# Attention in a four-layer decoder stack: value products of eight heads as one step, a 96-wide turned shift, and a mask taken by VectorE's minimum

## What is computed

```python
# layer 0: causal self-attention, cross-attention, feed-forward (1024)
# layer 1: causal self-attention, cross-attention, mixture of 8 experts, top 2
# layer 2: self-attention with a mask given as input, cross-attention, feed-forward
# layer 3: cross-attention
def _mha(x, ctx, wq, bq, wk, bk, wv, bv, wo, bo, mask):      # layer 2
    ...
    scores = jnp.einsum('bhqd,bhkd->bhqk', q, k) / np.sqrt(HEAD_DIM).astype(np.float32)
    if mask is not None:
        scores = jnp.where(mask == 0, NEG, scores)
    attn = jax.nn.softmax(scores, axis=-1)
    out = jnp.einsum('bhqk,bhkd->bhqd', attn, v)
    ...
```

## Time and profile before

| | |
|---|---|
| Time, median of 3 runs | 3417.2 us |
| The 3 runs | 3417.2, 3429.27, 3404.26 us |
| The profiled execution's own time | 3387.68 us |
| Its span, first to last instruction | 3385.9 us |
| PE busy in the span | 3120.8 us (92%) |
| DVE, ACT, POOL busy | 1568.8, 1541.6, 872.8 us |
| Mean granted clock of TensorE | 0.951 of full speed |

### The profile page before, as it was taken

The page is one execution under the profiler, slowest core; times in us unless marked ns, Lnnn a source line. Parts: engine busy times, 40 slices in busy tenths (PEclk is TensorE's granted clock), DMA queues, the critical chain, the costliest instruction groups (busy, mean ns, idle before and its releaser), DMA issues. The chain is left out here.

```text
span 3385.9 us, 61962 instructions
## 1 busy us (share of the span) xinstructions
PE 3120.8 (92%) x24016; PEld 2469.1 (73%) x24016; DVE 1568.8 (46%) x4051; ACT 1541.6 (46%) x3403; POOL 872.8 (26%) x991
## 2 busy tenths in 40 slices
PE   6899998999999999975999999789999999999996
PEld 5777776777877777764888888657676776777774
DVE  4544556645566555443100010275555555655542
ACT  3555455555556554442222222245555554555542
POOL 2112214222224222322000000332243433343332
PEclk8999999999999999995999999899999999999996
DMA  9725436455454453742766655553354565453321
GB/s 159 104 40 66 56 49 105 67 71 67 64 74 80 70 67 59 168 77 105 231 220 211 204 198 195 103 82 48 54 76 59 64 77 69 63 80 59 52 54 28
DMA packets 394608, 319.35 MB, mean 94 GB/s; under 512 B 151711, under 2 KB 378271, under 8 KB 394303
## 3 DMA queue, kind: packets, MB, share of 16 engines
q1 hardware_dynamic: 371062, 276.77, 46.7%
q0 software_dynamic: 8272, 23.73, 2.6%
q10 hardware_dynamic: 14981, 14.89, 1.4%
HBM read 134.33 MB, written 37.22 MB: 51 GB/s over the span
## 5 line engine op out<-in xcount | busy, mean ns | idle before, releaser
L1067 DVE TENSOR_REDUCE a_maxima<-a_bank 128x2 f32<-128x512 f32 (+3 forms) x576 | 342.4, 646 | 159.6 <-PE a_bank L690 158.9
L918 ACT ACTIVATE a_prob<-a_bank 128x512 f32<-128x512 f32 (+1 forms) x640 | 335.6, 603 | 157.9 <-PE a_bank L710 154.5
L954 ACT ACTIVATE b_group_hidden<-b_bank,b_b 128x256 f32<-128x256 f32 x312 | 131.0, 471 | 421.7 <-PE b_bank L776 421.7
L918 ACT ACTIVATE c_prob<-c_bank 128x512 f32<-128x512 f32 (+1 forms) x512 | 264.6, 599 | 112.6 <-PE c_bank L710 112.1
L1067 DVE TENSOR_REDUCE c_maxima<-c_bank 128x2 f32<-128x512 f32 (+1 forms) x448 | 260.4, 636 | 112.0 <-PE c_bank L690 110.8
L821 PE MATMUL a_bank<-a_causal_b,keep_identb 128*128 128x256 bf16 (+1 forms) x768 | 251.4, 327 | 46.2 <-DMA a_qs<-a_shift 19.1
L776 PE MATMUL b_bank<-b_group_xt,b_w 128*128 128x256 f32 x1248 | 284.3, 381 | 0.8 <-DVE b_group_xt L1108 0.8
L760 PE MATMUL b_bank<-b_w,b_group_hidden 128*128 128x256 f32 x1248 | 275.8, 379 | 0.9 <-ACT b_group_hidden L954 0.9
L760 PEld LDWEIGHTS b_bank<-b_w,b_group_hidden 128*128 128x128 f32 x1248 | 237.0, 190 | 33.5 <-ACT b_group_hidden L954 1.3
L776 PEld LDWEIGHTS b_bank<-b_group_xt,b_w 128*128 128x128 f32 x1248 | 235.6, 191 | 32.0 <-DVE b_group_xt L1108 1.2
L1113 DVE TENSOR_TENSOR b_group_y<-b_bank,b_b 128x512 f32<-128x512 f32 x39 | 27.0, 691 | 364.7 <-PE b_bank L760 364.7
(11 more groups left out here) (237 smaller groups left out, 6692.4 us busy)
## 6 DMA issues: line engine op xcount, KB each, us to landing
b_w<-in_L_xattn_e_w SPq DMA_DIRECT2D x78, 1024.0 KB, 7.2
a_qs<-a_parts_q SPq DMA_DIRECT2D x384, 128.0 KB, 4.9
c_qs<-c_parts_q SPq DMA_DIRECT2D x288, 128.0 KB, 6.9
a_ks<-a_parts_k SPq DMA_DIRECT2D x192, 128.0 KB, 6.0
c_ks<-c_parts_k SPq DMA_DIRECT2D x96, 128.0 KB, 5.9
b_group_x<-sorted_in SPq DMA_DIRECT2D x39, 256.0 KB, 6.6
sorted_out<-b_group_y ACTq DMA_DIRECT2D x39, 256.0 KB, 5.1
sorted_in<-a_zeros SPq DMA_DIRECT2D x8, 1024.0 KB, 9.7
```

Source lines behind the costliest of these rows:

```text
L918: act.activation(prob[0:rows, first:first + cols], bank[0:rows, 0, 0:cols], ACT.Exp, scale=SCALE).then_inc(k.own(s), 1)
L954: ins = act.activation(hidden[:, f, :], bank[:, 0, j * S:(j + 1) * S], ACT.Gelu, bias=b1[:, f:f + 1])
L1067: v.tensor_reduce(maxima[:, q:q + qn, h:h + n].rearrange("p q h -> p h q"), bank[:, 0, 0:cols].rearrange("p (j q n) -> p j q n", j=n, q=qn ...
```

## The change

Four things are changed.

1. The value products ("pv") of two groups, eight heads, become one step. It waits for the last exp of both groups and holds both prob tiles until it ends. The plan also counts 0.1 us for each change between pv and other PE steps. The pools are the same: still four prob tiles in phase a and three in phase c.
2. "turn_shift" turns 96 columns instead of 48. The weights are two neighbouring blocks of 48, the second of which is the next 128 queries' or, for the last, a block of zeros. The upper half of the result is not used.
3. "km" of attention 4 no longer opens its bank with the mask. After each exp, DVE takes the minimum of the probabilities with "kept", an f32 tile that holds 2^100 for a key that counts and 0 for one that doesn't (1 throughout for a query without any key). That is a new step "cut" for each of the 16 heads, with two f32 operands of 128x512 in SBUF, and pv waits for it in place of the exp. "qm" keeps its mask. "kept" is made once in phase b, in place of mask_k.
4. The table AHEAD is replaced by one with more entries, by kind and by attention, so the plan gives another order for phases a and c throughout.

```diff
         elif s.kind == "turn_shift":
...
             for q in range(QT):
-                ins = pe.matmul(bank[0:NPART * H, 0, q * P:(q + 1) * P], least["parts"][:, q, :, :].rearrange("p s h -> p (s h)"),
-                                k.identb, start=True, stop=True)
+                ins = pe.matmul(bank[0:2 * NPART * H, 0, q * P:(q + 1) * P],
+                                least["parts"][:, q:q + 2, :, :].rearrange("p q s h -> p (q s h)"), k.identb, start=True, stop=True)
...
         elif s.kind == "km":
...
-            if at in SELF:
+            if at in CAUSAL:
                 open_with_mask(pe, k, at, bank[:, 0, :], matmuls[0], 1)
...
         elif s.kind == "pv":
...
-            until.wait_ge(*done("exp", b, at, (g, len(key_units(at, g)) - 1)))
-            if g % 2 == 0:
-                until.wait_ge(*freed(s, "bank"))
...
+            until.wait_ge(*max(done("cut" if at in MASKED else "exp", b, at, (g, len(key_units(at, g)) - 1)) for g in groups))
+            until.wait_ge(*freed(s, "bank"))
+            last = len(key_tiles(at)) - 1
+            for base, g in zip((0, S), groups):
+                prob = tile(s, "prob0" if base == 0 else "prob1")
+                for kt, kn in enumerate(key_tiles(at)):
+                    for j in range(4):
...
+        elif s.kind == "cut":
+
+            first, cols = key_units(at, s.part[0])[s.part[1]][2]
+            block = tile(s, "prob")[:, first:first + cols]
+            until.wait_ge(*done("exp", b, at, s.part))
+            v.tensor_tensor(block, block, k.kept.rearrange("p a b -> p (a b)"), ALU.min).then_inc(k.own(s), 1)
...
+            columns = self.steps[k].kind == "pv"
+            if self.steps[k].engine == "tensor" and columns != in_columns:
+                in_columns, start = columns, max(start, free_at["tensor"] + 0.1)
...
-AHEAD = {"a": {"enters": -2.0, "turns": -0.6, "projs": 0.8, "values": -0.4, "scores": 0.1, "pvs": -0.5, "ends": 0.3, "outs": -0.9,
...
+AHEAD = {"a": {("shifts", 0): 0.1, ("shifts", 1): 2.4, "ends": 0.3, "enters": -1.1, "ffs": 8.0, ("gains", 2): 7.6,
...
```

125 lines of the change are left out of this document (76 added, 49 removed).

## The result

The changed kernel takes 3317.7 us (median of 4 runs, 3315.7 to 3320.7), beside 3411.1 us for the kernel before, run on the same chip. The ratio is 0.972, with a 95% interval of 0.968 to 0.976: 93 us faster by the medians, 82 to 110 by the interval. I had forecast 3301 us and a gain of 116.

The account below looks back on a forecast made before the run. PE's instruction stream was taken as the bound, busy 3120.8 of 3385.9 us. 99.1 us less work and 17 less waiting (30 from the order, minus 13 for cuts) make 116 off the 3417.2 median: 3301 us, range 3230 to 3365.

Parts of the forecast that it names:

- The work: PE's instruction time in phases a and c: mask 56.3, pv 22.5 and turned shift 20.3 us, 99.1 us less in sum.
- Runs of pv: PE, phases a and c: 299 uninterrupted groups of value products become 201, at 0.23 us each, -22.5 us.
- The km pairs then follow each other ... so they just stay hidden. I take nothing for this.: PE, attention 4 in phase c: without the mask, two 98 ns weight loads still fit each pair's 0.22 us; no cost.
- the mask's matmuls: PE, phase c: 256 matmuls of 0.22 us removed ahead of attention 4's km pairs, -56.3 us.
- The turned shift: PE: 111 turn_shift runs lose 0.09 us on entry and 0.12 of their own, partly passed to pv; -20.3 us.
- width makes no difference here: Weight loads on PE: 48-wide ones last 102 ns and 128-wide ones 98, so 96 columns were given no extra load time.
- The cuts: DVE, phase c: 256 minimum instructions of 0.69 us, making PE wait 0.8 us a sequence, 13 us in all.
- About 1 us of waiting stays if the landing takes as long as before.: PE's wait for the shift's DMA: 9.1 us of work covers a 10.0 us landing; 30 us gained over 12 waits.
- It replaces all lists.: New order of phases a and c: 30 us less waiting for the shift in phase c, nothing taken for phase a.
- The second rival: Phase a's idle 90 us mid-phase and 44 at its end shrink by a third: 50 us more, 3251 us; chance 0.15.
- the first (only the mask): Rival: changing weight width is free or only shifts, the order gives nothing, just 56 us come off: 3361 us; chance 0.10.
- The third rival: DVE and POOL contend over SBUF, cuts take 1.43 us, PE waits, 12.5 us lost each sequence: 3518 us; chance 0.06.

## Why the prediction was right, and where its steps failed

The time came inside the range, 17 us above the forecast. Not all of that is merit: on the scale of the traces the sum was 47 us too large. That it looks closer on the scale of the timed runs is luck: the profiled execution of before happened to be a fast one, 24 us under its median. I added up phase c's slots on PE's time line, each kind of slot priced at its lower quartile (pairs at 0.22 us), and put what lies above it under slower slots:

| phase c, us | before | after | difference | predicted |
|---|---|---|---|---|
| work | 1060 | 983 | -77 | -76 |
| slower slots (half clock, pairs at ACT's pace) | 69 | 88 | +19 | 0 |
| idle | 74 | 94 | +20 | -17 |

What is left of the phase, 16 and 15 us, is mostly the 12 us after PE's last matmul. Priced by single instructions instead of slots, the first two differences are -73 and +15, so they are good to some 4 us.

- **The work.** Right: -77 for -76. pv steps take 1.00 us for eight heads of a cross-attention and 1.87 for self-attention, 0.14 and 0.15 beyond 0.43 for each four matmuls, as priced. Runs of pv were not tried alone.
- **"The km pairs then follow each other ... so they just stay hidden. I take nothing for this."** This step failed. Weight loads do stay hidden, four pairs take 0.87 us. But twelve are held by the banks, 0.9 us for a steady sequence, some 14 in all if the others are like it. I had seen six exps take 3.04 us, 0.51 each, and should have set that beside 0.22: without the mask, PE outruns ACT more than twice over. Put back, the mask's matmuls cost 32 to 36 us, not 56.
- **The turned shift.** Right as far as the runs can tell: 16 us, 9 to 23, for 20, and the slot of 0.11 us. But "width makes no difference here" was the wrong reading of two loads of other shapes. A 96-wide load takes 24 ns longer than a 48-wide one. The Trainium skill's rule (TensorE: Matmul & The Clock Gate, "LDWEIGHTS (loading the stationary operand)") would make it 40 ns, and by it the gain would be 11, an estimate; the 24 ns lie between nothing and that rule, and the time measured cannot tell the three apart.
- **The cuts.** Size right (0.70 us each, 0.61 from one to the next, and 12 to 17 us in all for my 13). Place wrong: nothing in a steady sequence, all of it in the first stage.
- **"About 1 us of waiting stays if the landing takes as long as before."** This is the step that failed most. I counted PE's work behind the turn correctly and took the landing as given. The change had put twelve copies, 7.7 us of SP's queue, around the moment when the shift is ready, and the landing moved from 10.0 to 12.65 us. Instead of -30 it is +9 us of waiting for the shift in phase c, and another +9 in phase a, for which I had taken nothing. I had listed the order on PE, DVE and ACT, and not read SP's at this place.
- **"It replaces all lists."** I treated the order as a term of its own. It is none: 0 us alone, some 73 with the new work. The second rival (the order gives 50 us more than I can read) failed in its sum, the first (only the mask) in its premise. The third rival's mechanism exists and is small (below); PE never loses 7.3 us a sequence. But in the old order the cuts cost 44 us, so a chain behind the cuts was a danger, and the order removed most of it.
- **Open.** In the first stage of phase c, idle time and low clock grew by some 40 us. The cuts are 13 of it. The rest has no one name: four waits for the shift (7.5 us, before one of 2.9), and others that grew by a few us each. What the order is worth without the cuts, 45 us, has no name either. Issuing the shift on ACT did not shorten the stage.

## What to carry to other kernels

When work is taken off the busiest engine, list what then becomes late for each stretch, above all latencies that the work had covered, and read the queue of the engine that issues the DMA as closely as the busy one: a small urgent transfer may belong on another issuing engine than the bulk copies, as it did here in two kernels. Price an order together with the work that it orders, and expect steady sequences and the filling of the pipeline to answer differently. A pause costs more than itself, since the clock is low behind it.

## What the runs showed of the hardware that I had not expected

DVE's cuts slow POOL. In phase c, a POOL tensor_tensor of 512 columns takes 1396 ns on average in the changed kernel and 1272 without the cuts, and the issue of an indirect DMA 1114 against 997. All six traces of kernels without cuts, the kernel before among them, show 1270 to 1273 for the first, all eight with them 1350 or more:

```profile
L1304 POOL TENSOR_TENSOR c_tok<-c_tok,weights_row_L_xattn_ln_g 128x512 f32<-128x512 f32 x64 | 89.3, 1396 | 137.6 <-PE c_bank L681 136.8 <-DVE c_tok L1087 0.8
...
L1323 POOL DMA_INDIRECT c_pair_y<-sorted_out,keep_rows x64 | 71.3, 1114 | 210.1 <-POOLq L1421 192.4 <-issue 16.1 <-DVE c_tok L1165 1.3
```

The cut itself has a median of 684 ns and a longest of 1759. The Trainium skill (GPSIMD Engine Reference, the row on SBUF interfaces) names this contention, and the trace agrees; it makes 15 us of POOL's time, which nobody waits for.

One SP queue has a price that no busy row shows: 0.63 us for each copy. The 576 copies of parts in phase c are 36 for a sequence, so 23 us of a period of 68.6, and in order. At this place the order of the two costs PE 3.4 us (the shift behind the copies) or 5.5 us (the copies behind the shift).

The 24 KB of the shift took longer the more traffic was around them: the last packet was through 1.9 us after the issue with no copies ahead, 6.0 us with fewer copies ahead and on a queue of its own, and 6.9 us on one queue behind twelve copies of 128 KB.
